# Attention of a two-layer AdaLN kernel: scores, maxima and exponentials of a pass laid beside each other, and the far tokens' experts chosen ahead of the second pass' maxima

## The reference, cut to what matters

```python
def step(carry, i):                      # three passes
    qcur, prev, attn, cw, temp, done = carry
    qp = qcur @ lq_w.T + lq_b
    kp = k_full @ lk_w.T + lk_b
    vp = v_full @ lv_w.T + lv_b
    sq = _ln(qp, lnc_w) * tscale
    sk = _ln(kp, lnd_w)
    scores = jnp.einsum('bhqd,bhkd->bhqk', sq, sk) * inv_sqrt_e
    scores = jnp.where(in_win[None, None, None, :], scores, -jnp.inf)
    probs = jax.nn.softmax(scores, axis=-1)
    out = jnp.einsum('bhqk,bhkd->bhqd', probs, vp)
    iter_out = jnp.where(in_win[None, None, :, None], out, 0.0)
    diff = jnp.mean(jnp.abs(iter_out - prev))
    # queries += iter_out; the window cw grows or shrinks with diff
...
logits = xf @ router_w.T
topk_probs, topk_idx = jax.lax.top_k(jax.nn.softmax(logits, axis=-1), TOP_K)
```

## Time and profile before

| | |
|---|---|
| median of three runs | 455.07 us (452.31 to 455.73) |
| the profiled execution | 457.89 us |
| its span, from the first to the last instruction | 456.2 us |
| mean granted TensorE clock over the span | 0.75 of full |
| busy in the span: TensorE, VectorE, ScalarE, GpSimd | 305.5, 302.1, 171.8, 173.6 us |

### The profile page before, as it was taken

How to read it: one execution, slowest core, us unless ns; L and a number is a source line. 1 busy time by engine, 2 the same in 40 slices (tenths; PEclk the granted TensorE clock), 3 DMA queues, 4 the chain that set the end, 5 groups by cost and what they waited for, 6 DMA issues and landing times.

```text
span 456.2 us, 7413 instructions
## 1 busy us (share of the span) xinstructions
PE 305.5 (67%) x2070; PEld 221.0 (48%) x2071; DVE 302.1 (66%) x859; ACT 171.8 (38%) x331; POOL 173.6 (38%) x281
## 2 busy tenths in 40 slices
PE   2876886789926899697888999307716300689960
PEld 1662215333313332486887999303615300589960
DVE  7597976994779993278736565475888770377850
ACT  1144452217602167052425555647006600345520
POOL 9572870930233344302564455400000077044450
PEclk9986559555985558869889999856875555699995
DMA  2599700000000000031213221595000012323310
GB/s 77 105 368 361 206 3 0 1 1 1 13 18 29 23 25 25 24 54 54 56 51 71 63 65 37 154 282 166 1 1 1 0 63 105 94 70 74 94 50 0
DMA packets 37805, 32.93 MB, mean 72 GB/s; under 512 B 10765, under 2 KB 28770, under 8 KB 37776
## 3 DMA queue, kind: packets, MB, share of 16 engines
q1 hardware_dynamic: 33792, 25.10, 19.8%
q0 software_dynamic: 3936, 7.49, 5.2%
q10 hardware_dynamic: 48, 0.00, 0.0%
HBM read 19.50 MB, written 13.98 MB: 73 GB/s over the span
## 4 chain that ended last, share of the span: by engine, by line
PE 30%; DVE 25%; DMA 20%; issue 10%; ACT 5%; POOL 5%; SPq 2%; DVEq 1%; another core or an unknown queue 0%; POOLq 0%; ACTq 0%
DMA rows<-token_rows,posu 15%; PE ps L1237 9%; PE ps L1248 6%; POOL rows L585 4%; DVE mx L1765 3%; PE ps L1053 2%; PE ps L1028 2%; DVE stats L1373 2%; PE ps L1048 2%; DVE hb L1910 2%; SPq L293 1%; PE ps L1004 1%; DVE wide L2007 1%; PE ps L1205 1%; PE ps L1221 1%
## 5 line engine op out<-in xcount | busy, mean ns | idle before, releaser
L585 POOL DMA_INDIRECT rows<-token_rows,posu x48 | 51.9, 1080 | 147.1 <-DVE token_rows L1688 74.2
L1248 PE MATMUL ps<-w_out,hg 128*128 x496 | 67.2, 281 | 1.0 <-DVE ys L1921 0.7
L1910 DVE TENSOR_TENSOR hb<-ps,b_in 128x512 f32<-128x512 f32 x62 | 42.5, 686 | 36.2 <-PE ps L1237 31.3
L1248 PEld LDWEIGHTS ps<-w_out,hg 128*128 128x128 f32 x496 | 61.7, 196 | 1.8 <-issue 1.6
L597 POOL DMA_INDIRECT back<-ys,places x39 | 38.8, 995 | 52.0 <-DVE ys L1921 41.2
L866 ACT ACTIVATE hg<-hb 128x512 f32<-128x512 f32 x62 | 39.1, 630 | 41.4 <-DVE hb L1910 30.8
L1765 DVE TENSOR_REDUCE mx<-ps 128x2 f32<-128x512 f32 (+2 forms) x48 | 44.4, 949 | 5.4 <-PE ps L1028 5.1
L1237 PE MATMUL ps<-xsT,w_now 128*128 128x128 f32 x256 | 39.6, 304 | 10.1 <-issue 4.1
L1237 PEld LDWEIGHTS ps<-xsT,w_now 128*128 128x128 f32 x256 | 35.5, 214 | 12.3 <-issue 10.7
L1028 PE MATMUL ps<-feat,qs 64*128 64x281 bf16 (+2 forms) x128 | 33.3, 431 | 11.7 <-DVE mx L1765 7.3
L1221 PE MATMUL ps<-ident,xs 128*128 128x128 f32 x62 | 18.2, 297 | 32.5 <-DMA xs<-rows 32.2
(11 more groups left out here) (388 smaller groups left out, 546.3 us busy)
## 6 DMA issues: line engine op xcount, KB each, us to landing
rows<-blank SPq DMA_DIRECT2D x20, 260.0 KB, 6.1
xs<-rows SPq DMA_DIRECT2D x62, 64.0 KB
w_in<-in_L_ffn_w_fc SPq DMA_DIRECT2D x1, 2048.0 KB, 13.7
w_in<-in_L_ffn_W SPq DMA_DIRECT2D x1, 2048.0 KB, 10.5
rest<-rows SPq DMA_DIRECT2D x23, 65.0 KB
token_rows<-in_L_attn_x SPq DMA_DIRECT2D x1, 832.0 KB, 8.4
wmod<-in_L_wmod SPq DMA_DIRECT2D x2, 384.0 KB, 4.5
rows<-token_rows,posu POOLq DMA_INDIRECT x48, 2.3
```

The costliest lines, as they stand in the source:

```text
L585: pool.indirect_dma_start(ROWS[l], bass.IndirectOffsetOnAxis(ap=posu[:, k, j:j + 1], axis=0), token_rows[:, j, 0:WIDTH[l]], None).then_inc ...
L1248: mm = pe.matmul(ps[:, 6 + c % 2, 0:D], hg[:, c % RING, n * P:(n + 1) * P], w_out[:, bass.ds(e * NB + n, 1), :], start=(n == 0), stop=(n = ...
L1910: v.tensor_tensor(hb[:, c % 2, :].rearrange("p (b t) -> p b t", b=NB), ps[:, c % RING if h_bank(l, t) is None else h_bank(l, t), :].rearra ...
```

## The change

The new layout: the keys of a head are split (`KEY_PARTS`: 256 in pass 0, 170 and 111 in pass 1, 170 and 139 in pass 2) so that all query tiles of one part fit one bank; scores use banks 0 and 1 only, in turn, and each part has its own reduction (`mx` has two halves, and `stack_maxima` becomes a maximum of the two). Transposed scores of a head lie without gaps in two banks, 3 and 4 or 5 and 6, for which one of the three matmuls is cut in two where it crosses from one bank to the next. The turning uses banks 3, 4, 5, 6 at the start of a pass and bank 2 later (`TURN_AT`), the weighed values of all four groups bank 7, and so weighing group g waits until ScalarE has taken g - 1.

The new order: eight heads of scores, then by turns a head's transposed scores and another head's scores, with the turning of maxima and the weighing in between. Then the edits around it: `choose("far")` ahead of the maxima of pass 1; `count("far")` behind the last transposed scores of pass 1; the change of the output (`asum`) multiplied behind two turnings; and two far scatters in flight instead of one, on two semaphores (`scattered_far` and `scattered_odd`), both of which SyncE waits for in the end. Turning back the first three groups' outputs now comes together, ahead of the sixteenth head's weighing.

```diff
+KEY_PARTS = [[(a, min(a + 512 // -(-n // P), n)) for a in range(0, n, 512 // -(-n // P))] for n in WINDOWS]
+MAXIMA0 = [HEADS * sum(len(p) for p in KEY_PARTS[:it]) for it in range(3)]
...
-        LOGIT_AT = {"far": (5, 0), "near": (3, 0)}
-        COUNT_AT = {"far": ((7, 0), (7, 256)), "near": ((2, 0), (3, 256)), "all": ((3, 0), (4, 0))}
+        LOGIT_AT = {"far": (7, 0), "near": (3, 0)}
+        COUNT_AT = {"far": ((1, 288), (1, 400)), "near": ((2, 0), (3, 256)), "all": ((3, 0), (4, 0))}
+        TURN_AT = (3, 4, 5, 6, 2, 2, 2, 2)
+        def exponents(h, n):
+            b = 3 + 2 * (h % 2)
+            return ps[:, b:b + 2, :].rearrange("p a n -> p (a n)")[:, 0:n]
...
-                    pool.wait_ge(sem("scattered_far"), 16 * sent)
+                    pool.wait_ge(sem("scattered_far"), 16 * (sent - sent // 2))
+                    pool.wait_ge(sem("scattered_odd"), 16 * (sent // 2))
                     set_places(NA, NT, N)
                     pool.wait_ge(sem("places_set"), 3)
                 for j in range(NA, NT):
-                    if j > NA:
-                        pool.wait_ge(sem("scattered_far"), 16 * sent)
-                    send_row("far", 0, k, j)
+                    if sent > 1:
+                        pool.wait_ge(sem(("scattered_far", "scattered_odd")[sent % 2]), 16 * (sent // 2))
+                    send_row("far", 0, k, j, odd=bool(sent % 2))
                     sent += 1
...
+                stack_copy(it, 4)
+                exps(0, 3)
+                stack_copy(it, 5)
+                exps(3, 7)
+                take(0)
+                stack_copy(it, 6)
+                exps(7, 11)
+                take(1)
                 stack_copy(it, 7)
-                exps(2, 8)
-                take(0)
-                exps(8, 12)
-                take(1)
-                exps(12, 16)
+                exps(11, 15)
                 take(2)
+                exps(15, 16)
                 take(3)
...
-                def scores(lo, hi):
-                    for h in range(lo, hi):
-                        b = h % 2
-                        pe.wait_ge(sem("max_free"), H0 + h + 1)
+                def score(h):
+                    if h == 0:
+                        pe.wait_ge(sem("qs_first"), it + 1)
+                        pe.wait_ge(sem("ks_set" if it else "ks_act"), 2 * it - 1 if it else 4)
+                    elif h % 4 == 0:
+                        pe.wait_ge(sem("qs_act"), C0 + h // 4)
+                    if it and h == 4:
+                        pe.wait_ge(sem("ks_set"), 2 * it)
+                    parts = KEY_PARTS[it]
+                    for k, (lo, hi) in enumerate(parts):
+                        n = MAXIMA0[it] + len(parts) * h + k
+                        pe.wait_ge(sem("max_free"), n + 1)
                         for j in range(nj):
-                            mm = pe.matmul(ps[:, 3 * b + j, 0:nw], half(qs, h)[:, j * P:(j + 1) * P], half(ks, h)[:, 0:nw], start=True, stop=True)
+                            mm = pe.matmul(ps[:, n % 2, j * (hi - lo):(j + 1) * (hi - lo)], half(qs, h)[:, j * P:(j + 1) * P],
+                                           half(ks, h)[:, lo:hi], start=True, stop=True)
                         mm.then_inc(sem("s_ready"), 1)
...
-                def turn_maxima(g, copied):
-                    pe.wait_ge(sem("qs_act"), C0 + copied)
+                def turn_maxima(g):
                     pe.wait_ge(sem("max_stack"), G0 + g + 1)
-                    turn(g)
-                def scores_t(lo, hi):
-                    for h in range(lo, hi):
-                        b = h % 2
-                        if h < 2:
-                            pe.wait_ge(sem("max_free"), H0 + HEADS + 1 + h)
-                        else:
-                            pe.wait_ge(sem("probs_ready"), H0 + h - 1)
-                        if h % 4 == 0:
-                            pe.wait_ge(sem("qs_act"), C0 + 4 + h // 4)
-                        for j in range(nj):
-                            mm = pe.matmul(ps[:, 3 * b + j, 0:nw], half(ks, h)[:, j * P:(j + 1) * P], half(qs, h)[:, 0:nw], start=True, stop=True)
-                        mm.then_inc(sem("st_ready"), 1)
+                    pe.wait_ge(sem("qs_act"), C0 + 3 + g)
+                    turn(4 + g)
+                def score_t(h):
+                    if h >= 2:
+                        pe.wait_ge(sem("probs_ready"), H0 + h - 1)
+                    if h % 4 == 0:
+                        pe.wait_ge(sem("qs_act"), C0 + 4 + h // 4)
+                    e = exponents(h, 1024)
+                    for j in range(nj):
+                        a = j * nw
+                        cuts = [a, a + nw] if a // 512 == (a + nw - 1) // 512 else [a, 512, a + nw]
+                        for lo, hi in zip(cuts, cuts[1:]):
+                            mm = pe.matmul(e[:, lo:hi], half(ks, h)[:, j * P:(j + 1) * P], half(qs, h)[:, lo - a:hi - a], start=True, stop=True)
+                    mm.then_inc(sem("st_ready"), 1)
...
                     if jk == 0:
-                        if g < 2:
-                            pe.wait_ge(sem("qs_act"), C0 + 6 + g)
-                        else:
-                            pe.wait_ge(sem("o_taken"), G0 + g - 1)
-                        if it == 1 and g == 1:
-                            pe.wait_ge(sem("counts_read"), 1)
+                        if g:
+                            pe.wait_ge(sem("o_taken"), G0 + g)
                         pe.wait_ge(sem("probs_ready"), H0 + 4 * g + 4)
...
                 pe.wait_ge(sem("q_stack"), it + 1)
+                if it == 0:
+                    pe.wait_ge(sem("ks_act"), 4)
                 turn(0)
+                turn(1)
                 if it:
                     pe.wait_ge(sem("asum"), it)
-                    pe.matmul(ps[:, 3, 0:1], ones[:], asum[:], start=True, stop=True).then_inc(sem("change"), 1)
-                turn(1)
-                pe.wait_ge(sem("qs_first"), it + 1)
-                if it == 0:
+                    if it == 1:
+                        pe.wait_ge(sem("lg_read"), 1)
+                        pe.wait_ge(sem("ks_masked"), 2)
+                    pe.matmul(ps[:, 7, 0:1], ones[:], asum[:], start=True, stop=True).then_inc(sem("change"), 1)
+                else:
                     pe.wait_ge(sem("values"), 1)
-                    pe.wait_ge(sem("ks_act"), 4)
-                else:
-                    pe.wait_ge(sem("ks_set"), 2 * it - 1)
-                scores(0, 1)
+                turn(2)
+                turn(3)
+                for h in range(8):
+                    score(h)
+                    if h == 6:
+                        turn_maxima(0)
+                for h in range(HEADS):
+                    score_t(h)
+                    if h < 8:
+                        score(h + 8)
+                    if h % 4 == 2 and h < 11:
+                        turn_maxima(h // 4 + 1)
+                    g, k = divmod(h - 5, 4)
+                    if h >= 5 and k == 0:
+                        weigh_four(g, 0)
+                    elif h >= 5 and k == 1:
+                        weigh_four(g, 1)
+                        if nj == 3:
+                            weigh_four(g, 2)
                 if it == 1:
-                    pe.wait_ge(sem("lg_read"), 1)
-                    pe.wait_ge(sem("ks_masked"), 2)
-                scores(1, 2)
-                turn(2)
-                scores(2, 4)
-                pe.wait_ge(sem("qs_act"), C0 + 1)
-                turn(3)
-                if it:
-                    pe.wait_ge(sem("ks_set"), 2 * it)
-                scores(4, 8)
-                turn_maxima(0, 2)
-                scores(8, 12)
-                turn_maxima(1, 3)
-                scores(12, 16)
-                turn_maxima(2, 4)
-                scores_t(0, 2)
-                turn_maxima(3, 5)
-                scores_t(2, 6)
-                for g in range(3):
-                    weigh_four(g, 0)
-                    scores_t(4 * g + 6, 4 * g + 7)
-                    weigh_four(g, 1)
-                    scores_t(4 * g + 7, 4 * g + 8)
-                    if nj == 3:
-                        weigh_four(g, 2)
-                    if it == 1 and g == 0:
-                        count("far")
-                    if g < 2:
-                        scores_t(4 * g + 8, 4 * g + 10)
...
...
             def maxima(it):
                 nj, nw = -(-WINDOWS[it] // P), WINDOWS[it]
+                parts = KEY_PARTS[it]
                 def stack_maxima(g):
-                    v.wait_ge(sem("max_free"), 2 + HEADS * it + 4 * g + 4)
-                    v.tensor_copy(stack[:, 0:nj * HEADS, 1].rearrange("p (j h) -> p j h", h=HEADS)[:, :, 4 * g:4 * g + 4],
-                                  mx[:, 0:nj, 4 * g:4 * g + 4]).then_inc(sem("max_stack"), 1)
+                    v.wait_ge(sem("max_free"), 2 + MAXIMA0[it] + len(parts) * (4 * g + 4))
```

(22 more changed lines are left out.)

49 lines of the change are left out of this document (27 added, 22 removed).

## The result

Four runs of the changed kernel took 473.32, 470.78, 466.96 and 470.77 us, median 470.77; four of the one before, beside them, have a median of 453.78. The ratio is 1.0365 with a 95% interval of 1.0279 to 1.0451: slower by 3.7%, 17 us. I had forecast +11 us and 466.0, within 454.5 to 474. The direction held, the time lies within the range, and the loss came by the path that I had named. The size was half as large again (the interval runs from 12.7 to 20.5 us), and the clock's rise, which I had put at 116, came at 133; the later parts say which terms made it so. The profiled execution took 473.32 us, its span 471.6.

The account below looks back on a forecast made before the run. Two side-by-side chains, far scatter and attention, were taken to bound the kernel, with TensorE at half clock bounding the interleaving. +12.4 through pass 2 and -1 for the scatter gave +11.4, taken as +11: 455.07 + 11 = 466.0 us, range 454.5 to 474.

Parts of the forecast that it names:

- The shape: Attention and far scatter run side by side; scatter, 36 us, leaves the chain; in pass 1 the count decides, queries +10.1.
- The choice: Pass 1, moved ahead of the maxima: 13 VectorE instructions that nothing covers there, +3.8 us.
- Pass 0: First pass, interleaved: maxima end near 56.5, VectorE's idle cover is used up; -0.2 us, between -0.5 and +2.
- The turning ahead of the change's product: Pass 1, before the first reduction: a second turning ahead of the product for the output's change, +0.4 us.
- Eight heads, then eight steps: Pass 1: 10.0 us from first reduction to transposed scores, then interleaved steps with turnings and weighings at half clock, 18.3.
- The last eight heads: Pass 1, transposed scores and weighing: 9.8 us, between 12.9 at 1.2 GHz and half of it, clock up from about 116.
- Pass 2: Third pass: outputs at 200.5 against 188.08, +12.4; the pass itself loses 2.3, between -1 and +6.
- Behind attention: After the third pass' outputs: the scatter leaving the chain gives back little, -1 us, between -2 and 0.
- The split reductions: Passes 1 and 2: a head costs two reductions; in pass 1 1.15 us, plus 0.15 for the wait on the bank.
- The early clock: Rival, chance 0.17: gap-free interleaving in pass 1 brings 2.4 GHz soon after 98.9; 455 us.
- The row with 3.5 us without a gap at 0.50: Kernel before, 101.5 to 105: TensorE busy without a gap in scores and turnings, granted clock 0.50; cited against early clock.
- The scatter without overlap: Rival, chance 0.08: two far sends in flight land no faster, scatter ends at 207, +16 to +17; 472 us.

Follow-up runs that it names:

- before_pair: The kernel before with only the change's two far scatters in flight on two semaphores; median 455.7, ratio 1.000.
- after_single: The changed kernel with one far scatter in flight again, as before; median 470.7, ratio 1.033 to the kernel before.
- after_count_early: The changed kernel with the far count moved ahead, behind the last turning of maxima (head 10 of 16); median 467.0, ratio 1.022 to the kernel before.
- after_choose_late: The changed kernel with the far experts chosen behind the second pass' maxima again; median 462.4, ratio 1.013 to the kernel before.
- after_apart: The changed kernel without interleaving: all 16 heads' scores first, choice behind maxima, count behind head 6's transposed scores; median 472.7, ratio 1.037 to the kernel before.
- before_warm: The kernel before with four spare 128-row, 128-column matmuls behind each head's scores from the sixth on; 467.1, ratio 1.027.
- after_raise: after_both with long spare matmuls (512 columns) added in the second and third pass; 462.5, ratio 1.015 to the kernel before.
- after_best: The changed kernel with choice behind the maxima, count at head 12, and spare 512-column matmuls in all passes; 471.9, ratio 1.029 to the kernel before.
- after_pass1: The changed kernel with choice behind the maxima, count at head 12, and spare 512-column matmuls in pass 1 alone; median 461.03 beside 458.19 for the kernel before.
- after_both: The changed kernel with choice behind the maxima and count behind the last turning of maxima; median 461.5, ratio 1.013 to the kernel before.

## Why the prediction was right, and where its terms were off

**The shape.** Attention beside the scatter, scatter off the path, pass 1 as the place of the loss, the count as what releases the next queries, VectorE's 10.6 us from count to queries (132.51 to 143.09): each came as written, and before_pair and after_single measured the first two by themselves. Sends 36 us long were 37.

**The choice: +3.8 forecast, 5.5 measured** (86.41 to 91.87). The thirteen instructions were the same and the place was right, but I took their durations from where they stood before. There GpSimd was idle; here it was in its rotations. Three of the thirteen steps, of 0.27, 0.27 and 0.17 us, took 0.57, 0.64 and 1.20, and these three are the whole 1.7 us. The longest ended at 91.87, when this instruction of GpSimd ended too (91.85):

```profile
90.59 1.26 POOL L678 TENSOR_TENSOR rotx<-y 128x512 f32<-128x512 f32 x1
```

after_count_early has 5.5 for them too, beside the same GpSimd work, and after_choose_late, where they stand behind the maxima, 3.8 again. This is the term "+3.8".

**Pass 0: -0.2 forecast, +1.5 measured.** Maxima ended at 56.2 (I had 56.5) and VectorE was ready at 70.4 (70.9), but the outputs came 2.49 us later than that. I had looked at VectorE's cover and taken the outputs for early. In the changed kernel's profiled execution the clock stayed at half through all of pass 0. In after_count_early and after_single, with the same instructions, it rose at 65.5 and the outputs came in time (70.6); so the +1.5 says more of one execution than of the edit.

**The turning ahead of the change's product: +0.4 forecast, 0.0 measured.** From outputs to first reduction, less the choice, is 13.5 us in both kernels.

**Eight heads, then eight steps: 28.3 us forecast, 26.5 measured.** First reduction to transposed scores was 10.3 (10.0), and the steps with turning and weighing 16.2 (18.3): 102.19 to 118.37. A step without them was 1.5 and not 1.7: I had 0.81 for the transposed scores of a head, which took 0.68, and somewhat more for its scores, which took 0.84.

**The last eight heads: 9.8 forecast, 13.7 measured** (118.37 to 132.06). This is the term that failed: "with the clock up from about 116 on". It stayed at half until 133. The 12.9 that I had worked out for half clock and not taken would have been near, and the rest is a term that I left out: the third turning of maxima also falls among these heads (121.75 to 122.50, 0.75 us), and 12.9 and 0.75 are the 13.7. In the kernel before the clock had risen in the second group's weighing (115), and I put the rise into the same work without a row that showed scores between it. Why it came later stays open.

Together: 1.7 for pass 0, 1.7 for the choice, -0.4 for the turning, -1.8 for the steps, 3.9 for the last eight give the count at 132.1 instead of 127.0, and that is the whole error up to the count. Pass 2 was forecast at 62.4 and was 64.0, by the same term: its last eight heads took 11.1 us (187.93 to 199.04) and not 9.3, the clock having risen at 187.5; its other terms lie within 0.5. Behind attention I had -1 and it was -0.1 to the first expert and -3.5 after it. Of that I only know that it is there, and that before_pair has 2.5 of it with the paired sends alone. My sum foresaw 1 us of these 3.6; without the other 2.6 the time would have been 473.4, within a microsecond of the range's upper bound, and that it wasn't is luck.

**What I left out.** The split reductions were in the sum (1.30 a head; the kernel before takes 1.11), but as part of the interleaving. I never asked what the layout would cost by itself, since the price was to be covered by the overlap. With all scores ahead it is 4.9 us in pass 1 and 6.0 in pass 2, and after_apart is the run that shows it: with this layout the interleaved order is the faster one. How much of the changed kernel's own 17 us is the layout, no run separates, since there only eight heads' scores stand ahead.

**The rivals.** The early clock (455) didn't come by itself. The row with 3.5 us without a gap at 0.50 was borne out: before_warm has 13.00 busy us of 13.00 at 0.50. The Trainium skill ("TensorE: Matmul & The Clock Gate", section "What's actually happening") says that sustained activity releases the throttle. In these 13 us the trace disagrees with it. Rises came at other places: 4 and 8 us behind the first score with long spare matmuls between (after_raise, after_best), and just ahead of the first score without any (after_pass1). But the mechanism of the rival is real. Where the clock was up and choice and count were back (after_best, after_pass1), the second pass took 55.4 and 53.3 us, less than the 56.6 before the change. The scatter without overlap did not happen. By its own terms it would have cost 5 us on top of the forecast (215 against 210 for the first expert), and one send in flight cost 4.0 in after_single's trace.

## What to carry to other kernels

A chain of waits shows one of several chains that end together; before shortening its largest entry, look for what else ends within a few us of it. When work is laid beside other work, ask first which engine is to carry both, at the clock that it has there and not at the one that it has elsewhere, and price the new layout alone, without the overlap that is to pay for it. Durations of a moved instruction belong to the place it came from: look at what the other engines do in the new one. And before a term is read from one execution, look how far the same instructions lie apart in two.

## What the runs showed of the hardware

- TensorE at 100% busy for 13 us (before_warm, 97 to 110) kept 1.2 GHz, with 64-row scores and short full-height matmuls between them. With three of 512 columns behind each head, 2.4 GHz was granted 4 us after the first score (after_raise, 82.6 to 87) or 8 us after it (after_best, 86.4 to 94.5), and in pass 2 of after_best not within 16 us.
- The same instructions on TensorE found 2.4 GHz in pass 0 at 59.5, 65.5, 65.5 or 71 us, or not at all, in seven kernels; after_pass1 had it at 85.0 where the changed kernel, alike up to there, had it at 133.
- Once up, the clock held through interleaved scores and transposed scores with spare work (after_best, 94.5 to 132). It went down where TensorE had waited 1.5 to 2 us for another engine (after_raise at 111 and 158.5, after_both at 119.5), and also where its longest wait in the 6 us before had been 0.83 us (after_pass1 at 115.5).
- Beside busy GpSimd, three of thirteen small VectorE instructions took 0.57, 0.64 and 1.20 us for 0.27, 0.27 and 0.17, and the row of thirteen 5.5 for 3.8.
- Indirect scatters with two in flight followed each other 1.48 us apart, one at a time 2.8 us, with nothing else slower that a measurement tells (before_pair, 1.000).
